# Routing in nine and seven batches, first tiles begun in the last two batches: a fused attention and expert kernel

## The reference, cut to what matters

```python
h = rms(x, ln1_w[l]); q, k, v = h @ wq[l], h @ wk[l], h @ wv[l]     # 16 heads of 64, 4 key heads
x = clip(x + softmax(rope(q) @ rope(k).T / 8 + causal) @ v @ wo[l])
h = rms(x, ln2_w[l])
topv, topi = top_k(softmax(h @ wr[l]), 2)                           # 2 of 8 experts for each row
x = clip(x + sum(w_e * ((silu(h @ wg[l, e]) * (h @ wu[l, e])) @ wd[l, e])))
```

## Time and profile before

| | |
|---|---|
| median of 3 runs | 2183.49 us (2180.12 to 2187.3) |
| the profiled execution | 2187.7 us, span 2185.9 us |
| TensorE busy | 2040.0 us, 93% of the span |
| VectorE, ScalarE, GpSimd busy | 61%, 47%, 24% |
| mean granted TensorE clock | 0.977 of 2.4 GHz |

### The profile page before, as it was taken

One profiled execution on the slowest core, in us unless ns is written; L12 is line 12 of the kernel. 1 busy time (PEld: TensorE's weight loads), 2 busy tenths in 40 slices (PEclk: granted clock), 3 DMA queues, 4 the chain that ended last, 5 costly groups with the idle time before them and its releaser, 6 DMA issues.

```text
span 2185.9 us, 34265 instructions
## 1 busy us (share of the span) xinstructions
PE 2040.0 (93%) x9801; PEld 1514.6 (69%) x9802; DVE 1323.1 (61%) x2944; ACT 1025.1 (47%) x3727; POOL 521.0 (24%) x624
## 2 busy tenths in 40 slices
PE   5768999989999999989999999989999999989994
PEld 4646788766666888766667878766667887766662
DVE  4655787864336778754335887744346878844345
ACT  2211666653333676653233667652334676543231
POOL 2212332242003222143012222232011322332013
PEclk8879999999999999999999999999999999999997
DMA  6510233022112232022121222022121331022123
GB/s 185 164 47 18 91 101 100 5 77 77 51 44 59 76 116 88 1 80 87 44 59 48 100 100 71 31 61 79 47 65 35 104 120 46 13 83 72 44 69 96
DMA packets 90870, 156.08 MB, mean 71 GB/s; under 512 B 13746, under 2 KB 64516, under 8 KB 90628
## 3 DMA queue, kind: packets, MB, share of 16 engines
q1 hardware_dynamic: 74836, 113.07, 16.3%
q0 software_dynamic: 15904, 41.38, 6.5%
HBM read 108.22 MB, written 46.18 MB: 71 GB/s over the span
## 4 chain that ended last, share of the span: by engine, by line
PE 64%; DVE 18%; ACT 8%; issue 4%; POOL 3%; DMA 1%; DVEq 0%; SPq 0%; POOLq 0%; ACTq 0%
PE ps L815 22%; PE ps L834 11%; ACT parena L1099 7%; DVE rope L1433 6%; PE ps L713 6%; PE ps L786 5%; PE ps L735 3%; PE ps L824 3%; PE ps L750 2%; PE ps L721 2%; POOL qk L526 2%; PE ps L688 2%; DVE qk L1421 2%; DVE rmax L1443 2%; PE ps L809 1%
## 5 line engine op out<-in xcount | busy, mean ns | idle before, releaser
L815 PE MATMUL ps<-arena,xeT 128*128 x1120 | 527.9, 594 | 6.1 <-ACT xeT L1137 4.4
L1099 ACT ACTIVATE parena<-ps,nmax 112x112 f32<-112x112 f32 x1024 | 344.6, 385 | 121.4 <-DVE nmax L1444 121.4
L815 PEld LDWEIGHTS ps<-arena,xeT 128*128 128x128 f32 x1120 | 203.4, 192 | 147.2 <-issue 140.5
L526 POOL TENSOR_TENSOR qk<-qk,rope 128x448 f32<-128x448 f32 x128 | 148.6, 1161 | 649.5 <-DVE rope L1433 649.3
L713 PE MATMUL ps<-xnT,wqk_s 128*128 128x224 f32 x1280 | 275.5, 359 | 8.8 <-ACT parena L1099 8.0
L1147 ACT ACTIVATE parena<-ps,er 128x512 f32<-128x512 f32 x140 | 96.2, 687 | 396.0 <-PE ps L815 392.2
L493 POOL DMA_INDIRECT y_in<-sorted_y,pos x150 | 143.3, 955 | 552.6 <-DMA sorted_y<-tarena 420.0
L834 PE MATMUL ps<-arena,tarena 128*128 x1120 | 265.0, 380 | 0.8 <-ACT tarena L1153 0.8
L1099 ACT ACTIVATION_READ_ACCUMULATOR parena<-ps,nmax 112x1 f32 x1024 | 245.1, 239 | 0.0
L713 PEld LDWEIGHTS ps<-xnT,wqk_s 128*128 128x128 f32 x1280 | 234.5, 193 | 13.9 <-ACT parena L1099 11.3
L735 PE MATMUL ps<-qk 128*112 128x224 f32 x1024 | 240.6, 358 | 0.0
(11 more groups left out here) (186 smaller groups left out, 2758.8 us busy)
## 6 DMA issues: line engine op xcount, KB each, us to landing
xe<-sorted_x SPq DMA_DIRECT2D x140, 130.0 KB, 2.1
sorted_y<-tarena SPq DMA_DIRECT2D x140, 128.0 KB
arena<-in_L_ffn_wg_dram SPq DMA_DIRECT2D x32, 512.0 KB, 3.6
arena<-in_L_ffn_wu_dram SPq DMA_DIRECT2D x32, 512.0 KB, 4.6
arena<-in_L_ffn_wd_dram SPq DMA_DIRECT2D x32, 512.0 KB, 5.5
arena<-in_ctx_dram SPq DMA_DIRECT2D x16, 375.0 KB
sorted_x<-tarena POOLq DMA_DIRECT2D x8, 568.8 KB, 5.7
sorted_y<-tarena POOLq DMA_DIRECT2D x8, 560.0 KB, 4.6
```

The costliest lines, as they stand in the source:

```text
L526: pool.tensor_tensor(q, q, rope[m % 2][:, :], ALU.add).then_inc(g_rope, 1)
L815: last = pe.matmul(ps[:, bank, :], xeT[u][:, k, :], w[:, bass.ds(e * 1024 + k * 512, 512)], start=(k == 0), stop=(k == KD - 1))
L1099: last = act.activation(prob[:, n, :], ps[0:S, bank, h * S:h * S + S], ACT.Exp, bias=nmax[:, b % 2, n:n + 1], scale=SCALE, accum_out=rsum[ ...
```

## The change

The parts become batches 0 to 8 and 9 to 15. From this follow `RANK_STEP` 10, `WHOLE` 8, `FIRST` 23. The routing arrays get memory of their own (`route`), so that `choose` no longer depends on `y_in`. VectorE's routing steps are cut into pieces and put elsewhere: `choose` of the first part between the maxima and the scaling of batch 10; the tiles in two pieces, one at the end of batch 10, one (`starts_of_first`) in the same gap of batch 11; `place_first` in two pieces, at the end of batch 11 and in the gap of batch 12; `gates` in batch 13. GpSimd scatters batches 0 to 2 ahead of the one rotation of batch 12, batches 3 to 6 ahead of the three of batch 13, and 7 and 8 after them. In odd batches `top_two` comes behind the last rotation, and in even ones `take_logits` stands inside rotation 0. Tiles 0 and 1 are both turned at the end of batch 14; in batch 15 TensorE multiplies gate and up of tile 0 and the gate of tile 1. Tile 1 then has the turn of batch 15's row (`turn_x`) behind its up product and `route_logits` behind `down`. The second part is counted in tile 2 and placed ahead of tile 3. Two short loops over tile pairs are unrolled. In the first stage `sorted_y` is no longer zeroed (the first layer's gathers, whose weights are zero, read two stored rows), and the eight stores to `sorted_x` are issued in batches 8 to 15.

The diff, cut to its core:

```diff
-PARTS = ((0, 10), (10, 16))
+PARTS = ((0, 9), (9, 16))
+        route = sb("route", [S, (4 * PN * TOPK + 1) * E + PN * TOPK])
-            return y_in[:, :, :, :].rearrange("p u k d -> p (u k d)")[:, at[0] - width:at[0]]
+            return route[:, at[0] - width:at[0]]
-        ZERO_STORES = 2 * (HROWS // rows)
+        ZERO_STORES = HROWS // rows
...
 # GpSimd
-                if i < len(zeroed):
-                    t, n = zeroed[i]
+                if i >= ZERO_FROM:
+                    n = i - ZERO_FROM
-                        in_=sorted_y[0:FIRST * SLOT, :] if b < PARTS[0][1] else sorted_y,
+                        in_=sorted_y[0:2, :] if l == 0 else sorted_y[0:FIRST * SLOT, :] if b < PARTS[0][1] else sorted_y,
-            SOONER = (0, 2, 3, 4)
+            SOONER = (3, 7)
                         for m in (2, 3, 4) if odd else (1,):
                             if b == RANK_STEP + 2:
-                                scatter_first(l, SOONER[m - 2:m])
+                                scatter_first(l, 0, SOONER[0])
+                            if b == RANK_STEP + 3 and m == 2:
+                                scatter_first(l, *SOONER)
                             add_rotated(l, g + 1, m)
...
 # TensorE, iteration(b)
+                        if b == B - 1:
+                            pe.wait_ge(m_xT, l * NT + 1)
                         scores(l, b, 0)
+                        if b == B - 1:
+                            pe.wait_ge(m_xT, l * NT + 2)
                         scores(l, b, 1)
...
                         else:
-                            turn_tile(0, 0, 1, 1)
+                            pe.wait_ge(ld_mw, (l + 1) * 16 * 3 * E)
+                            pe.wait_ge(d_te, l * 2 + 1)
+                            up(0, 0, expert_of(0), wg_s, 0, m_g)
...
                     elif odd:
-                        pe.wait_ge(m_xT, l * NT + 1)
-                        up(0, 0, expert_of(0), wg_s, 0, m_g)
+                        up(0, 0, expert_of(0), wu_s, 1, m_u)
...
-                    elif odd:
-                        up(0, 0, expert_of(0), wu_s, 1, m_u)
+                    else:
+                        pe.wait_ge(a_exp, l * 32 + 2 * b + 2)
+                        if odd:
+                            up(1, 1, expert_of(1), wg_s, 2, m_g)
+                        else:
+                            for T in range(2):
+                                turn_tile(T, T, 1, 1 + T)
...
-                turn_tile(1, 1, 1)
                 turn_hidden(0, 0)
                 out_project(B - 1)
                 tile(1, 1, 2, first=True)
-                pair(1)
-                pe.wait_ge(d_lg, (l + 1) * B)
-                count_rows(1, 7)
-                pair(2)
-                with pe.Fori(3, WHOLE // 2) as i:
+                tile(2, 0, 2, count=True)
+                tile(3, 1, 3)
+                for i in range(2, WHOLE // 2):
                     pair(i)
...
 # VectorE, iteration and tiles
+                    if b == RANK_STEP:
+                        choose(0)
+                    if b == RANK_STEP + 1:
+                        starts_of_first()
+                    if b == RANK_STEP + 2:
+                        place_first(1)
                     scale_probs(b, 0)
...
-                            rotate(step, l, g + 1, 0, 1 if b else 2)
-                    if b:
+                            rotate(step, l, g + 1, 0, 1 if b else 2, between=take_logits)
+                    if b and (odd or g + 1 == NP):
                         take_logits(b - 1)
...
+                    if odd and g + 1 < NP:
+                        rotate(step, l, g + 1, 4, 2)
                     if b:
                         top_two(b - 1)
-                    if odd and g + 1 < NP:
-                        rotate(step, l, g + 1, 4, 2)
...
-                tile(2, 0, 1)
-                choose(1)
+                tile(2, 0, 1, count=True)
+                place_second()
                 tile(3, 1, 2)
-                copy_ranks(1, 7)
-                tiles_of_second()
                 tile(4, 0, 2)
-                place_second()
+                experts_of_later()
                 tile(5, 1, 3)
-                experts_of_later()
                 gates(1)
```

More of the change, by code:

```diff
@@ L418, in layer_io @@
                 pair(1, pieces=True)
-                with sp.Fori(2, WHOLE // 2 - 1) as i:
+                for i in range(2, WHOLE // 2 - 1):
                     pair(i)
@@ L449, in _ @@
             pool.wait_ge(z_ready, 6)
-            zeroed = [(t, n) for n in range(HROWS // rows) for t in (sorted_x, sorted_y)]
-            assert len(zeroed) <= B
+            ZERO_FROM = B - ZERO_STORES
+            assert ZERO_FROM >= 0
             def norm_factors(out, var, n, at=0):
@@ L930, in iteration, with tile @@
                             norm_turn(l, g + 2, k, 4, k * TN)
[L932 removed]
+                def tile(T, u, n, first=False, early=False, end=False, count=False):
                     e = expert_of(T)
[L934 to L935 removed]
+                    if not first:
+                        pe.wait_ge(m_xT, l * NT + T + 1)
                         pe.wait_ge(m_h, l * NT + T - 1)
[L938 to L941 removed]
+                        up(T, u, e, wg_s, 2 * u, m_g)
                         turn_hidden(T - 1, 1 - u)
+                    if count:
+                        pe.wait_ge(d_lg, (l + 1) * B)
+                        count_rows(1, 7)
                     if early:
@@ L952, in tile @@
                     down(T - 1, 1 - u, expert_of(T - 1))
+                    if first:
+                        route_logits(B - 1)
                 def pair(i):
@@ L1435, in rotate @@
                 if m == 0:
-                    step(ins)
+                    if between and g > 1:
+                        ins.then_inc(step.sem, 1)
+                        step.n += 1
+                        between(2 * g - 3)
+                        dve.wait_ge(step.sem, step.base + step.n)
+                    else:
+                        step(ins)
                     ins = dve.tensor_tensor(rope[0][:, :], out_c, rope[0][:, :], ALU.add)
@@ L1682, in early, with tile @@
                         rows_in(step, n, at)
-                def tile(T, u, n, first=False):
+                def tile(T, u, n, first=False, count=False):
                     hidden(T, u)
+                    copy_factors(T + 1, 1 - u)
                     if first:
```

45 lines of the change are left out of this document (18 added, 27 removed).

## The result

| | before | after |
|---|---|---|
| median of 4 runs | 2184.56 us (2180.12 to 2187.3) | 2130.56 us (2129.83 to 2131.27) |
| ratio, 95% interval | | 0.9752 [0.974, 0.9764] |
| span of the profiled execution | 2185.9 us | 2129.1 us |
| TensorE busy | 2040.0 us, 93% | 2026.2 us, 95% |

The account below looks back on a forecast made before the run. TensorE, busy 93%, bounds the kernel, so only its idle time can go: 51.6 less 9.6 coming back, plus 3.3, less 1.2, is 44.1 us. From 2187.7 that gives 2143.6, as median 2139; range 2128 to 2160, its own 2129 to 2149.

Parts of the forecast that it names:

- the 51.6 us: The most the change could remove inside the layers: 44.8 us of listed TensorE waits plus 6.8 of slowed clock.
- 0.8 comes back, with the rotation 1.2 a layer: Batch 12: 0.8 us of TensorE wait returns because the count moved; 1.2 a layer with the rotation, bounds 0.3 and 2.0.
- the reorders: Logits sooner in even batches, last rotation sooner in odd ones: 11.3 us of waits go, 2.0 (0 to 5) return.
- the 0.98: TensorE's wait of 0.98 us at 918.35 in batch 12 before the change, behind VectorE's late maxima.
- GpSimd's scatters: Fourteen scatters and one rotation take 19.0 us, over by 937.8, so the 3.38 us wait for GpSimd goes whole.
- the second rival: Scatters slower where VectorE is busy: 6.9 us for fourteen, a 4.9 us wait before batch 14's scores; 2165, chance 0.06.
- the third rival: Eight scatters ahead of three rotations delay them; slower from 2.1 us a scatter on, 2195 at 2.3; chance 0.03.
- The first two tiles: Turn of tiles 0 and 1 after batch 14: 0.8 us in hand, 0.2 a layer booked, bounds 0 and 1.5.
- The second part: Rows of batches 9 to 15 come late for tile 8: TensorE waits 0.5 us a layer, bounds 0 and 3.4.
- The first stage and the end: Load of `x` ends 3.3 us sooner without two stores of zeros; last layer's gather of batch 9 is 1.2 later.
- the first four: Second part's rows late, 2151 (0.12); slow scatters, 2165 (0.06); scatters delaying rotations, 2195 (0.03); waits only move, 2181 (0.03).
- The fifth case: All of the 51.6 us and the first stage's 4.3 gone: 2126, chance 0.03.

## Why the prediction was right, point by point

**What bounds the kernel, and the 51.6 us.** Right: TensorE's own idle time was what went, at the places listed. Three things were off. The 17 short waits of L733 had the one of 1.1 us ahead of the layers among them, which stayed. The clock cost 3.4 us in layer 2, not 1.7 (its windows of 10 us show 0.66 at 1430, the others 0.83 to 0.87), so 8.5 instead of 6.8. And some 6 us that the list doesn't hold went as well: the four layers gave 53.6 us in all, where listed waits and clock, less the 4.3 that came back, make 47.9.

**Where the 12.7 us lie.** 9.6 us were to come back and 4.3 did: 5.3. The clock is 1.7, the end of the last layer 1.0, the first stage 0.1. The other 4.6 are the time outside the list, less the 1.1 that stayed. So the forecast, which lies in its range, is right by mechanism, and its errors all went the same way.

**Routing in VectorE's gaps.** The step that failed here is "0.8 comes back, with the rotation 1.2 a layer". Nothing came back in batch 12. The last rotation ended 0.75 us behind the start of the scores, with 0.77 before (the row at 909.24 and scores at 909.72, now 888.97 and 889.48), though TensorE no longer spends 1.3 us on the count there: the top two (0.6) stands behind the rotation now, and the second half of the scaling starts 0.6 sooner against TensorE's turns. I had booked the first with the reorders and left it out of this sum. From rotation to maxima it is 2.7 instead of 3.7 us, and so the 0.98 is gone to the last hundredth. What did come back is 0.39 us a layer at 932.50, a place that I had not listed. The likely reason, which no run tests: with two turns of tiles instead of heads or values, TensorE has less between the probabilities' first and second half.

**GpSimd's scatters.** Right in mechanism and nearly in size. The fourteen and one rotation took 19.97 us for 19.0 (898.39 to 918.36). The 1.0 more is scatters that began under VectorE's scaling: that of 912.61 took 1.81 us, while the scaling ran from 912.51 to 913.60, so it ended 0.82 behind it. All three slow ones of a layer began under a scaling, and none of the sixteen of the four layers that began under a maximum from PSUM was slow (in the kernel before four of twelve took 1.05). The scaling has both inputs in SBUF. The Trainium skill says in "SBUF — State Buffer", section "SBUF: two separate sides", that a VectorE step with two SBUF inputs and a GpSimd step that reads SBUF take the shared ports in turn, and that the later one blocks until the other is over. The trace agrees: each slow scatter ended 0.8 to 0.9 us behind the scaling, at 1.4 us for fourteen scatters. This is the second rival's mechanism at a fifth of its price (6.9), and the third rival's 2.1 us a scatter was never near.

**The first two tiles.** Right: no wait; 0.2 a layer had been booked.

**The second part.** Right in mechanism, at the turn that was named: 0.5 a layer was booked, 0.5 to 1.0 measured, 2.7 in all for 2.0.

**The reorders.** The step that failed most: "VectorE's own chain was already about as long as TensorE's, so I let 2.0 come back". Nothing did. The rule that stood beside it (the mix free again, 0.36 us) gave 2137, nearer the mark, but not for its reason: with the top two behind the maxima the mix is long again and nothing comes back either. The run with the reorders alone shows 11.7 us in batches 0 to 9 for the 9.3 booked, and 7 more behind, mostly by the clock.

**The first stage and the end.** The copy behind the wait for `x` comes 2.6 us sooner, for 3.3, and the wait is 1.90 us where about 1 was named. By the first output turn it is 3.4 (253.0 to 249.6), but that this is so near to 3.3 is luck: in the changed kernel's three profiles that turn stands at 248.2, 249.1 and 249.6. At the end the gather of batch 9 was issued 5.0 us behind the start of the last product instead of 4.1, as foreseen; but from that product to the end it is 33.3 us for 33.1, and 33.9 in the second profile of the changed kernel. The chain of gathers took up most of the 1.2.

**The rivals and the signs.** None of the first four happened. Of the signs, the waits of about 1 us in batch 12 did not come, and the wait for `x` was 1.90; the others came as named. The fifth case, all of the listed waits gone, 2126, got 0.03; 2130.6 lies between it and the forecast, nearer to it, and what came back at tile 8 and 932.50 is about as much as what is between. The chance was too small: each term of what would come back was taken at a middle value of its bounds, and for most of them the trace held a reason for the lower end.

## What to carry to other kernels

Two short waits that stand in the same loop may be one lateness: sum them, ask which instruction is ahead of both, and price that one. Look at the single durations of a repeated instruction by place in the loop, not at median and longest; a step that is slow in every second pass hides in a median. And a small independent step between a GpSimd sum and the next VectorE step on SBUF data can be free, where removing it gains nothing. Where a wait ends for no reason that the view names, look up when the semaphore rose and whose it is, before calling it a stop of the engine that waits.

## What was not expected of the hardware

- VectorE's TENSOR_SCALAR on 112x256 f32 took 0.35, 0.73 or 1.33 us beside GpSimd's sum (1.13), and the SCALAR_TENSOR_TENSOR behind it 0.48 or 1.24. A start 0.05 us ahead of the sum gave 0.35 in four cases and 1.32 in one.
- The granted clock does not follow from one wait's length. In the run with the reorders alone it stayed at 1.00 behind 3.39 us in two layers, fell behind the same wait in a third, and fell behind one of 2.00 in the fourth. With six scatters ahead it fell behind waits of 1.0 to 1.1 us one close behind the other, in three layers.
- A scatter of 0.94 us took 1.13 to 1.82 when it began under VectorE's scaling (both inputs in SBUF, 1.09 us), twelve times of twelve in the changed kernel; in the kernel before nine of ten took over 1.0.
- On two of three chips the semaphores of TensorE rise up to 10.0 us behind the end of its records while GpSimd issues fourteen or more scatters in a row, some 45 us of 2175 in all; on the first chip never over 0.03.
